# Attention: two of each sixteen subtractions of the probabilities' high parts move from GpSimd to VectorE

## What is computed

```
q, k, v = split(layernorm(x) @ W_qkv);  ql, kl = q, k through low-rank maps of 32 per head
scores = where(causal, (ql * lsr_core) @ kl^T / sqrt(32), -inf)
attn = softmax(scores)
y = (attn @ v) @ W_o;  x = x + y
```

## Time and profile before

| | |
|---|---|
| median of three runs | 2342.39 us |
| the profiled execution's own time | 2342.5 us |
| its span, first to last instruction | 2340.8 us |
| busy: TensorE, VectorE, ScalarE, GpSimd | 71%, 79%, 63%, 57% |
| attention: first and last subtraction | 1152.8 us and 1762.7 us |
| subtractions on GpSimd | 512, mean 918 ns |
| `maxima` on VectorE | 512, mean 552 ns |

### The profile page before, as it was taken

One profiled execution on the slowest core, in us unless ns is written; L12 is line 12 of the kernel. 1 busy time (PEld: TensorE's weight loads), 2 busy tenths in 40 slices (PEclk: granted clock), 3 DMA queues, 4 the chain that ended last, 5 costly groups with the idle time before them and its releaser, 6 DMA issues. The chain is left out here.

```text
span 2340.8 us, 52167 instructions
## 1 busy us (share of the span) xinstructions
PE 1654.0 (71%) x16780; PEld 1352.2 (58%) x16780; DVE 1857.7 (79%) x4943; ACT 1471.0 (63%) x3849; POOL 1342.9 (57%) x1496
## 2 busy tenths in 40 slices
PE   4676675766657369995689999999986459998000
PEld 2444454454546158884488888888875338887000
DVE  6999999999978957776689999999975867776221
ACT  5666676766743647774388888888883457776000
POOL 3545555555540045554399999999971035553774
PEclk8778787777865679998699999999995579999555
DMA  1000001010034013333122222222214013333232
GB/s 29 14 14 22 20 14 28 14 27 14 19 104 140 1 48 81 81 80 58 39 57 57 57 59 59 59 57 57 57 28 129 23 27 81 81 81 67 74 80 57
DMA packets 188967, 122.59 MB, mean 52 GB/s; under 512 B 24320, under 2 KB 177824, under 8 KB 188704
## 3 DMA queue, kind: packets, MB, share of 16 engines
q1 hardware_dynamic: 154016, 75.18, 11.6%
q0 software_dynamic: 17408, 35.69, 6.9%
q10 hardware_dynamic: 17280, 8.40, 1.2%
HBM read 66.22 MB, written 44.04 MB: 47 GB/s over the span
## 5 line engine op out<-in xcount | busy, mean ns | idle before, releaser
L1044 POOL DMA_INDIRECT ffn_xs<-normed,ffn_tokeni x288 | 273.1, 948 | 460.1 <-DVE posi L1420 260.7
L1877 POOL TENSOR_TENSOR att_pl<-att_p,att_ph 128x384 f16<-128x384 f32 x512 | 455.3, 918 | 56.3 <-ACT att_ph L2098 48.6
L323 POOL TENSOR_TENSOR sq<-states,qS 128x256 f32<-128x256 f32 x256 | 250.9, 980 | 304.3 <-DVE states L733 303.3
L543 ACT ACTIVATE decayed<-states,alpha 128x64 f32<-128x64 f32 x1024 | 272.3, 336 | 177.6 <-DVE states L733 175.7
L379 PE MATMUL bank<-sq,ident 128*128 128x128 f32 x1024 | 249.9, 415 | 93.4 <-POOL sq L323 93.4
L2206 DVE TENSOR_REDUCE att_mx<-bank 128x3 f32<-128x384 f32 x512 | 279.9, 552 | 41.0 <-PE bank L1934 36.8
L1251 ACT ACTIVATE ffn_h<-bank,b_cols 128x256 f32<-128x256 f32 x576 | 226.4, 475 | 127.7 <-PE bank L1139 117.4
L379 PEld LDWEIGHTS bank<-sq,ident 128*128 128x128 f32 x1024 | 220.0, 240 | 128.9 <-POOL sq L323 100.7
L2095 ACT ACTIVATE att_p<-bank 128x384 f32<-128x384 f32 x512 | 252.2, 493 | 58.9 <-PE bank L1971 55.5
L2098 ACT ACTIVATE att_ph<-bank 128x384 f16<-128x384 f32 x512 | 253.0, 494 | 0.0
L1152 PE MATMUL bank<-w_h,ffn_hh 128*128 x1152 | 225.6, 223 | 14.9 <-DVE ffn_hl L1439 4.5
(11 more groups left out here) (336 smaller groups left out, 5085.5 us busy)
## 6 DMA issues: line engine op xcount, KB each, us to landing
slots<-ffn_ys SPq DMA_DIRECT2D x144, 128.0 KB
ffn_x_all<-x SPq DMA_DIRECT2D x16, 512.0 KB, 4.8
normed<-ffn_xn ACTq DMA_DIRECT2D x32, 256.0 KB, 2.3
att_qz<-att_qp SPq DMA_DIRECT2D x256, 32.0 KB
ffn_xs<-normed,ffn_tokeni POOLq DMA_INDIRECT x288
xin<-in_x SPq DMA_DIRECT2D x64, 64.0 KB, 2.0
xres<-in_x SPq DMA_DIRECT2D x64, 64.0 KB, 2.0
x<-x SPq DMA_DIRECT2D x64, 64.0 KB, 1.8
```

The lines of the kernel that those rows point to most:

```text
L323: nc.gpsimd.tensor_tensor(sq[:, t, :].rearrange("p (h i j) -> p h i j", h=HL, i=D), states[:, t, :].rearrange("p (h i j) -> p h i j", h=HL ...
L543: ins = nc.scalar.activation(decayed[:, 64 * h:64 * h + 64], states[:, (t - 1) % TC, 64 * h:64 * h + 64], ACT.Copy, scale=alpha[p][:, t, h ...
L1044: pool.indirect_dma_start(xs[j % AHEAD][:, r, :], None, A["normed"], bass.IndirectOffsetOnAxis(ap=tokeni[:, BR * j + r:BR * j + r + 1], ax ...
L1877: nc.gpsimd.tensor_tensor(pl[:, h % RP, :], p32[:, h % RP, :], ph[:, h % RP, :], ALU.subtract).then_inc(low_done, 1)
```

## The change

In every step VectorE makes `pl` of head 3 and of head 11, at the very end of its slots 5 and 13. GpSimd skips them. The instruction is the same, on another engine. A new semaphore counts VectorE's two, and a helper `low_written` chooses which semaphore TensorE's `pv` and ScalarE's `exps` wait on.

```
+DVE_LOW_AT = {3: 5, 11: 13}
...
+        def low_written(eng, b, h):
+            b, h = b + h // H, h % H
+            if h in DVE_LOW_AT:
+                eng.wait_ge(low_dve, b * len(DVE_LOW_AT) + sorted(DVE_LOW_AT).index(h) + 1)
+            else:
+                eng.wait_ge(low_done, b * (H - len(DVE_LOW_AT)) + sum(k not in DVE_LOW_AT for k in range(h + 1)))
...
-                    pool.wait_ge(high_done, b * H + h + 1)
-                    nc.gpsimd.tensor_tensor(pl[:, h % RP, :], p32[:, h % RP, :], ph[:, h % RP, :],
-                                            ALU.subtract).then_inc(low_done, 1)
+                    if h not in DVE_LOW_AT:
+                        pool.wait_ge(high_done, b * H + h + 1)
+                        nc.gpsimd.tensor_tensor(pl[:, h % RP, :], p32[:, h % RP, :], ph[:, h % RP, :],
+                                                ALU.subtract).then_inc(low_done, 1)
...
-                pe.wait_ge(low_done, b * H + h + 1)
+                low_written(pe, b, h)
...
-                    act.wait_ge(low_done, b * H + h - RP + 1)
+                    low_written(act, b, h - RP)
...
+                    for low in DVE_LOW_AT:
+                        if DVE_LOW_AT[low] == h:
+                            dve.wait_ge(high_done, (NBUF * i + p) * H + low + 1)
+                            v.tensor_tensor(pl[:, low % RP, :], p32[:, low % RP, :], ph[:, low % RP, :],
+                                            ALU.subtract).then_inc(low_dve, 1)
```

More of the change, by code:

```diff
@@ L1700, in attention @@
         (ready, cleared, front_dve, front_act, front_pe, proj_pe, proj_act, proj_dve, maxi_dve, maxi_pe, tail_dve, tail_pe,
-         tail_act, s_ps, max_done, st_ps, exp_done, high_done, low_done, pv_done) = (
+         tail_act, s_ps, max_done, st_ps, exp_done, high_done, low_done, pv_done, low_dve) = (
             sem(n) for n in ("ready", "cleared", "front_dve", "front_act", "front_pe", "proj_pe", "proj_act", "proj_dve",
                              "maxi_dve", "maxi_pe", "tail_dve", "tail_pe", "tail_act", "s_in_psum", "max_done",
-                             "st_in_psum", "exp_done", "high_done", "low_done", "pv_done"))
+                             "st_in_psum", "exp_done", "high_done", "low_done", "pv_done", "low_dve"))
         ps_s, ps_st, ps_y, ps_x = bank[0:2], bank[2:4], bank[4:6], bank[6:8]
```

## The result

The changed kernel takes 2457.18 us (median of 4 runs, 2452.08 to 2462.16) against 2342.36: ratio 1.0491 [1.0468, 1.0515]. The sign was forecast; the size (2349.5, range 2338 to 2373) was not. The profiled execution took 2462.16 us, with a span of 2460.2.

The account below looks back on a forecast made before the run. The prediction took a loop from VectorE's slot 8 through `rows0` and DMAs to TensorE's next step as binding. 29 steps x 0.26 = 7.5 us, less 0.4 at the end, gave +7.1: median 2349.5 us, range 2338 to 2373.

Parts of the forecast that it names:

- The sign: Whole kernel: slower, with chance 0.63; same 0.25, faster 0.12.
- What bounds the kernel: Attention step: a loop through VectorE's slots 8 to 11, DMAs and TensorE's next step; less GpSimd work alone buys nothing.
- a delay ahead of slot 8: VectorE before slot 8: counts only once the slack is used up; 0.26 us a step expected on the loop.
- The moved subtraction: Head 3, slot 5 on VectorE: waits 0.5 us for GpSimd's head 5, ends 0.49 behind it, takes 0.9 to 1.1.
- The `maxima` of slot 6: VectorE behind head 3's subtraction: start moves from 1411.59 to 1412.51, that is 8.49 us into the step.
- Head 11: Slot 13 on VectorE: price 0, covered by idle time and TensorE's DMA wait; otherwise up to 0.5 us a step.
- `maxima` of slot 8: VectorE, slot 8: start 10.65 us into the step instead of 10.39, 0.26 us on the loop; steps take 19.4 us.
- the adds of slot 6: VectorE's two residual adds: no GpSimd subtraction running by then, so 0.34 + 0.34 - 0.08 us instead of 1.02.
- the rule that I had stated: Shared port: a VectorE instruction with two SBUF inputs waits until GpSimd's subtraction is over, then needs only its own data.
- the lost race: Rival, chance 0.18: in slot 6 GpSimd's head 6 starts before the second add; 2360 to 2397 us.
- the forecast mechanism: Slots 5 to 8: VectorE's wait for GpSimd delays the loop 0.26 us a step; +7.1 us in all.
- hidden: Rival, chance 0.25: the slot-5 instruction costs only 0 to 0.15 us on the loop; 2341 to 2347 us.

Follow-up runs that it names:

- head4c: Changed kernel, but VectorE takes head 4 instead of head 3, in slot 6 behind the adds: 2253.64 us against 2253.37 before in the same session, ratio 1.0000.
- yield6: Changed kernel, but GpSimd waits ahead of head 6's subtraction until the second residual add is done: 2351.20 us against 2341.81 before the change, ratio 1.0043.
- only11: Kernel before with only head 11's subtraction moved to VectorE, head 3 staying on GpSimd: 2346.18 us, ratio 1.0016 to the kernel before.
- busy: Changed kernel plus 24 unused matmuls on TensorE in slot 8, where it would wait for k01: 2428.22 us against 2343.71 before the change, ratio 1.0352.
- extra1: Kernel before plus one unused reduction on VectorE at the end of slot 5, no subtraction moved: 2347.14 us against 2342.22, ratio 1.0019.
- extra2: Kernel before plus two unused reductions on VectorE at the end of slot 5, no subtraction moved: 2454.40 us against 2341.81, ratio 1.0485.
- late3: Changed kernel, but VectorE makes head 3's low half in slot 6, behind the adds: 2353.40 us against 2342.22 before the change, ratio 1.0051.

## Why the prediction was wrong

**Right, and shown.** What bounds the kernel, as far as tested: 1.4 us less work on GpSimd gave nothing (head4c, 19.13 us a step), and a delay ahead of slot 8 counts once the slack is gone. It counted for more than was said: the step of yield6 grew by 0.26 us for a shift of 0.17, where the forecast had 0.26 for 0.26. Where the other 0.09 arise isn't known. The moved subtraction takes 1.00 us and ends 0.41 us behind GpSimd's head 5 (forecast 0.49). The `maxima` of slot 6 comes at 8.43 (8.49). Head 11 costs nothing in a regular step (only11). If the adds are let through, the `maxima` of slot 8 is at 10.56 (10.65), the step at 19.43 (19.4), and the whole at +9.4 us (+7.1) (yield6).

**The step that failed** is the sentence on the adds of slot 6: "There a wait goes away: by then GpSimd has no subtraction running, so they need 0.34 + 0.34 - 0.08 instead of 1.02." No subtraction is running, that is true. But one is released and queued behind the gather, and the port goes to it. The add at 0.66 us into the gather waits for the rest of the gather and for two whole subtractions. Even by the rule that I had stated, the first add would have ended before head 6 began. It was the rule, read out of one case, that was too narrow: I took it that VectorE waits for the subtraction that runs when it arrives.

**The rival that came nearest** was the lost race, with 0.18. It had only the second add in it, at most 1.9 us a step and 2397 us in all, since it too gave the first add the port. The earlier trace rows had the other answer in it: there an add waited 1.65 us through two subtractions in a row, though it had come first for the second. I priced that as a tail, and the change made it the rule: 2.41 + 0.99 in 23 of 29 steps.

**What was missing altogether** is the clock. A wait of 2.87 us on TensorE wasn't in any rival, so neither was a fall of its clock after one. In the kernel before, its pauses in a step were 0.6 and 0.5 us.

**The account.** By the ratios, 10 us are the forecast mechanism (yield6), 72 are the held adds (between yield6 and busy) and 33 the clock (between busy and the changed kernel). These three are steps of one chain, so they add up to the 115 by themselves. The steps shown bear them out: 2.74 us between yield6 and busy are 74 us in 27 steps, 1.12 between busy and the changed kernel are 30. Of the rivals, "hidden" is refuted by yield6 and the changed kernel; "GpSimd sets the pace" by head4c and by GpSimd's new idle time.

**Open.** Whether single steps like those of only11 and extra1 are all of the 0.2% by which these two are above the kernel before; and why in step 1721.87 the adds passed. There GpSimd started the gather 0.05 us behind the first add, after an idle time of 0.86 us that the profile puts down to the issue; what made that gap isn't known.

## What to carry to other kernels

Before an instruction is moved onto an engine that shares a port with its old one, look at what follows it there: every later instruction that needs the port gets a new place against the other engine's queue, and its place counts more than the sum of busy times. One extra reduction cost 5 us, two cost 113. Busy time of a waiting engine hides this (the adds rose from 61 to 122 us of VectorE's "work"); compare the same line's shortest and longest duration instead. If a wait of some us is about to appear on TensorE, price its clock afterwards too. And pick the piece to move by its deadline and by who stands behind it: head 4 behind the adds cost nothing, head 3 ahead of them 5%.

## What the runs showed of the hardware

**Who gets the port.** A count over the traces of all thirteen kernels, of VectorE instructions with two SBUF inputs that wait while GpSimd's subtractions follow each other. It gives how long before the end of the running subtraction the next one was released (its exponential done), and who came next:

```
next one released        VectorE next   GpSimd next
0.24 us or more before              0           154
0.20 to 0.24 us                    31            14
0.08 to 0.20 us                    90             1
```

So GpSimd keeps the port from one instruction to the next if the next is ready early enough, however long VectorE has waited. The same goes across a gather: with a subtraction released behind it, a VectorE instruction that started up to 0.27 us after the gather's start ran freely. Residual adds that came from 0.37 us on were held to the end of the gather and beyond, all 111 of them in these traces (extra2 at 0.45, the changed kernel at 0.66), and one already at 0.28 (only11). VectorE's subtraction in late3 still ran freely at 0.42. So the border lies somewhere in this stretch, and what sets it isn't known. With none released behind it the gather held nothing (yield6, at 0.66). Once free, VectorE ended an add 0.16 us after GpSimd's instruction. The Trainium skill, page "SBUF — State Buffer", section "Who interferes with whom", has a lock that whoever issues first holds for one instruction; here the add started 0.46 us before head 6's subtraction and was held by it, so in this case the measurement decides. How the choice is made inside was not tested.

**The clock.** After an idle time of 2.87 us TensorE's granted clock was 0.51 for 3.40 us, and the step lost 1.1 us by it; 27 such stretches stand in the attention; with 24 unused matmuls in that place it stayed at 1.00.

**The gather** took 1.10 us where VectorE's subtraction was running at its start, and 0.96 otherwise.
